# Sixteen-head cross attention: the order of the row tile groups on TensorE, and the bank that the weighed values are collected in

## The reference

```python
scores = jnp.einsum('bhqd,bhkd->bhqk', Q, K) / scale        # (8, 16, 100, 361)
attn = jax.nn.softmax(scores, axis=-1)
out = jnp.einsum('bhqk,bhkd->bhqd', attn, V)                # (8, 16, 100, 16)
out = out.transpose(0, 2, 1, 3).reshape(B, L, D) @ Wo + bo
```

## Time and profile before

| | us |
|---|---|
| median of three runs | 1513.96 |
| the profiled execution | 1514.17 |
| its span in the trace | 1512.4 |
| main loop of `l0x`, first to last turned maxima | 79.1 |
| the same of `l1x` | 79.6 |
| the same of `l3x` | 80.3 |

### The profile page before, as it was taken

One profiled execution on the slowest core, in us unless ns is written; L12 is line 12 of the kernel. 1 busy time (PEld: TensorE's weight loads), 2 busy tenths in 40 slices (PEclk: granted clock), 3 DMA queues, 4 the chain that ended last, 5 costly groups with the idle time before them and its releaser, 6 DMA issues. The chain is left out here.

```text
span 1512.4 us, 31527 instructions
## 1 busy us (share of the span) xinstructions
PE 1380.3 (91%) x12488; PEld 1067.8 (71%) x12488; DVE 777.7 (51%) x1733; ACT 644.3 (43%) x1683; POOL 194.8 (13%) x200
## 2 busy tenths in 40 slices
PE   7999899989989899899999889989958897899897
PEld 6776668866557588778999765669945676688632
DVE  3666677755556577520000466501127484576665
ACT  3444226643367356344444345432225674266300
POOL 3000250000024200040110420040042000300000
PEclk9999999999999999999999988999989995999999
DMA  6000340011301200366996100545221000700100
GB/s 214 2 1 1 68 68 16 3 43 42 79 8 21 47 9 3 105 230 246 340 345 247 48 22 1 202 186 200 73 55 37 1 2 1 112 9 3 67 1 22
DMA packets 43943, 120.19 MB, mean 79 GB/s; under 512 B 11931, under 2 KB 28440, under 8 KB 38412
## 3 DMA queue, kind: packets, MB, share of 16 engines
q1 hardware_dynamic: 33048, 62.04, 14.2%
q0 software_dynamic: 7616, 53.12, 10.1%
q10 hardware_dynamic: 3136, 3.03, 0.7%
HBM read 95.78 MB, written 11.00 MB: 71 GB/s over the span
## 5 line engine op out<-in xcount | busy, mean ns | idle before, releaser
L827 PE MATMUL wide<-early_kt,early_q 32*100 32x361 f32 x512 | 107.5, 507 | 2.8 <-PEq L66 1.6
L2558 ACT ACTIVATE l1f_hidden<-wide,l1f_pack 128x128 f32<-128x128 f32 x160 | 58.8, 368 | 78.0 <-PE wide L2497 68.1
L2680 DVE TENSOR_TENSOR l1f_out<-summed,l1f_pack 128x256 f32<-128x256 f32 x20 | 8.5, 424 | 152.9 <-PE summed L2505 152.9
L113 PE MATMUL summed<-ident 128*128 128x128 f32 x302 | 45.6, 319 | 33.3 <-PEq L66 33.3
L2497 PEld LDWEIGHTS wide<-l1f_rt,l1f_pack 128*128 128x128 f32 x640 | 74.5, 192 | 1.7 <-issue 0.8
L2497 PE MATMUL wide<-l1f_rt,l1f_pack 128*128 128x128 f32 x640 | 74.8, 275 | 0.6 <-ACT l1f_rt L2548 0.6
L2505 PE MATMUL summed<-l1f_pack,l1f_hidden 128*128 128x256 f32 x320 | 72.4, 379 | 0.0
L113 PEld LDWEIGHTS summed<-ident 128*128 128x128 f32 x302 | 43.3, 231 | 40.0 <-issue 40.0
L1223 DVE TENSOR_REDUCE l3x_mx<-wide 100x2 f32<-100x722 f32 x64 | 57.8, 907 | 14.7 <-PE wide L827 14.5
L1223 DVE TENSOR_REDUCE l1x_mx<-wide 100x2 f32<-100x722 f32 x64 | 57.8, 907 | 14.0 <-PE wide L827 14.0
L2505 PEld LDWEIGHTS summed<-l1f_pack,l1f_hidden 128*128 128x128 f32 x320 | 59.2, 190 | 7.2
(11 more groups left out here) (605 smaller groups left out, 3397.8 us busy)
## 6 DMA issues: line engine op xcount, KB each, us to landing
l2f_w<-l2f_w_dram SPq DMA_DIRECT2D x16, 1024.0 KB, 11.6
ctxt<-ctxt_dram SPq DMA_DIRECT2D x4, 1083.0 KB, 17.2
early_kt<-soon_kd SPq DMA_DIRECT2D x32, 90.8 KB, 3.3
l1f_sorted_x<-l1f_zeros SPq DMA_DIRECT2D x4, 640.0 KB
l1f_rows<-l1f_sorted_x SPq DMA_DIRECT2D x20, 128.0 KB, 7.7
l1f_sorted_y<-l1f_out ACTq DMA_DIRECT2D x20, 128.0 KB, 9.3
l0f_w<-l0f_w_dram SPq DMA_DIRECT2D x18, 128.0 KB, 2.1
l1f_shared<-l1f_shared_dram SPq DMA_DIRECT2D x1, 2180.0 KB, 8.2
```

Of the source, the lines that this page charges most:

```text
L113: pe.matmul(net.summed[:, 1, 0:P], net.ident[:], net.ident[:], start=True, stop=True)
L827: pe.matmul(wide[0:S, i, 0:SKV], q4[R * i:R * (i + 1), g % 2, b, g // 2, :], kt[R * i:R * (i + 1), g % 2, b, g // 2, 0:SKV], start=True, s ...
L2558: act.activation(hidden[:, f, 0:P], wide[:, f % 4, 0:P], ACT.Gelu, bias=b1_of(pack[:, n % SLOTS, :], f)).then_inc(sem["h_ready"], 1)
L2680: dve.tensor_tensor(out[:, n % 2], summed[:, n % 2, 0:E], b2_of(pack[:, n % SLOTS, :]), ALU.add).then_inc(sem["y_ready"], 1)
```

## The change

On TensorE, iteration n becomes: turned maxima of n; `score(n + 1, 1)`; `score_by_key(n - 1, (0, 1))`; `score(n + 2, 0)`; `score_by_key(n - 1, (2, 3))`; `weigh(n - 2)`. Both halves of the scores by key are now one quad behind, `weigh` stands last, and the mapping `TURN` is gone: turn i is head i. `weigh` writes into `scored[3]` instead of `scored[0]` and waits for the exponentials of its own quad only. On ScalarE `take(n - 1)` stands ahead of the fourth exponential of quad n instead of `take(n - 2)` behind the first. The turned maxima stay where they were, in bank 2 of `wide`.

```diff
-    TURN = (2, 3, 0, 1)
...
                     for c in range(NCH):
-                        for j in turns:
-                            i = TURN[j]
-                            last = pe.matmul(scored[j][0:CH, c * S:(c + 1) * S], kt[R * i:R * (i + 1), g % 2, b, g // 2, c * CH:(c + 1) * CH],
+                        for i in turns:
+                            last = pe.matmul(scored[i][0:CH, c * S:(c + 1) * S], kt[R * i:R * (i + 1), g % 2, b, g // 2, c * CH:(c + 1) * CH],
                                              q2[R * i:R * (i + 1), n % 2, :], start=True, stop=True)
                             if c == NCH - 1:
-                                last.then_inc(t_psum[j % 2], 1)
+                                last.then_inc(t_psum[i % 2], 1)
                 def weigh(n):
-                    pe.wait_ge(sem["p_ready"], min(Q * (n + 1) + 1, Q * QUADS))
+                    pe.wait_ge(sem["p_ready"], Q * (n + 1))
...
-                        for j in range(Q):
-                            i = TURN[j]
-                            last = pe.matmul(scored[0][i * V:(i + 1) * V, LOW:LOW + S], v1[0:rows_of(c), b, c, (Q * g + i) * W:(Q * g + i) * W + V],
-                                             pt[0:rows_of(c), (Q * n + j) % 8, c, :], start=c == 0, stop=c == NCH - 1)
+                        for i in range(Q):
+                            last = pe.matmul(scored[3][i * V:(i + 1) * V, LOW:LOW + S], v1[0:rows_of(c), b, c, (Q * g + i) * W:(Q * g + i) * W + V],
+                                             pt[0:rows_of(c), (Q * n + i) % 8, c, :], start=c == 0, stop=c == NCH - 1)
...
                     if 1 <= n <= QUADS:
+                        score_by_key(n - 1, (0, 1))
+                    if n + 2 < QUADS:
+                        score(n + 2, 0)
+                    if 1 <= n <= QUADS:
                         score_by_key(n - 1, (2, 3))
                     if n >= 2:
                         weigh(n - 2)
-                    if n + 2 < QUADS:
-                        score(n + 2, 0)
                     if n == 0:
                         keep_busy(pe, net, 3)
-                    if n < QUADS:
-                        score_by_key(n, (0, 1))
...
-                    act.activation(sums[:, n // NQ, n % NQ, :], scored[0][:, LOW:LOW + S], ACT.Copy).then_inc(sem["sums_ready"], 1)
+                    act.activation(sums[:, n // NQ, n % NQ, :], scored[3][:, LOW:LOW + S], ACT.Copy).then_inc(sem["sums_ready"], 1)
...
-                for n in range(QUADS + 2):
+                for n in range(QUADS + 1):
                     if n < QUADS:
-                        exps(n, (0,))
-                    if n >= 2:
-                        take(n - 2)
+                        exps(n, (0, 1, 2))
+                    if n >= 1:
+                        take(n - 1)
                     if n < QUADS:
-                        exps(n, (1, 2, 3))
+                        exps(n, (3,))
```

## The result

The changed kernel took 1497.61 us (median of four executions, 1495.78 to 1500.19), the kernel before, beside it on the same chip, 1513.81 (1509.19 to 1515.53): a ratio of 0.9896 with a 95% interval of 0.9858 to 0.9934. That is 16.2 us less; 14.3 were forecast, and 1499.7. Run again against 24 executions of the kernel before, it gave 0.9918 (0.9889 to 0.9947), 1497.66 us. The time is where it was expected. The trace says that it did not come from where it was expected throughout: two of the three loops gained nearly what was forecast, the third gained nothing, and two stages that the change does not touch made up for it.

What follows compares the result with a forecast made beforehand. PE's own list sets the pace: 2.534 us a quad falls to 2.37, 0.164 times 29 quads is 4.8 us a loop, three loops 14.3, ends cancelling: 1514.17 - 14.3 = 1499.9, or 1499.7 from the median; range 1495 to 1509.

Steps and rivals of the forecast that it cites:

- PE's list: TensorE's work per quad: turned maxima 0.23, both halves 1.48, weighing 0.65, together 2.36 us, 2.47 at the upper end.
- the pattern that iteration 1 had shown: In the kernel before, iteration 1 lacks a weighing; the next half's weights load 0.65 after the half before began, not 0.82.
- the wait for `highest(n + 1, 0)`: `score(n + 2, 0)` waits between the halves for VectorE's maxima, due at 0.86 to 0.90; row groups come free at 0.88.
- The three loops that are close: Loops of waits per quad on PE, DVE and ACT: 2.36, 2.34 and 2.30 us; 2.37 taken, 0.01 above the longest.
- VectorE's loop: DVE's way from one turned maxima to the next, through `with_maxima` and `highest`: 2.34 us a quad.
- The ends: Start and end of each main loop: 0.92 us gained, 0.92 lost, set off with 0.5 us either way.
- The third loop: The loop of `l3x`: 4.8 us gain like the others; its existing delays left as they are, 1 us in the range.
- A: Rival: a wait halves the gain, by PE's upper end or a longer ACT loop; 6 to 8 us, 1506 to 1508; chance 0.14.
- ScalarE's loop: ACT's loop through `take`, fourth exponential, scores by key and weighing: 2.30 us a quad, reserve 0.06 against PE's.
- B: Rival: row groups do not run past one another, a quad stays 2.53, nothing is gained, 1514 us; chance 0.08.
- C: Rival: second-half scores by key wait in program order; quad 2.81, 24 us more, 1538 us; chance 0.08.
- the 1.07 that the prediction names: Start of scores by key for (2, 3) after the turned maxima from which C decides; 0.92 to 1.01 was expected.

Runs made afterwards that it cites:

- halves apart: The changed kernel with the turned maxima put between the two halves, all else as changed: 1514.06 us, 1.0004 against the kernel before.
- VectorE out of the way: The changed kernel with VectorE's maxima taken over the first 181 of 361 keys only: 1491.26 us, 0.9831 against the kernel before.
- the wrong bank: The changed kernel with the weighing put back into `scored[0]`, with the waits that this needs: 1520.51 us, 1.005 against the kernel before.
- keys after eight quads: The changed kernel with SP issuing the last key transfers of `l3x` only after the scores of eight quads: 1498.88 us, 0.9883.
- keys ahead: The changed kernel with keys of batches 2 and 3 issued before queries in `l3x`, their tiles cleared earlier: 1504.4 us, then 1494.4 us.
- two copies: The changed kernel with ScalarE's `take` cut into two copies of 64 partitions each: 1529.96 us, 1.013 against the kernel before.

## Why the prediction was right, and where it was not

- **PE's list**: the mechanism is right, and the number is in part luck. 0.23 + 1.48 + 0.65 was forecast, 0.23 + 1.47 + 0.65 measured (1.50 in every other quad), in the pattern that iteration 1 had shown. With the halves apart it is 2.54 again. But with VectorE out of the way the halves take 1.43: PE's list alone is 2.32 or less, and what makes it 2.35 to 2.39 is the wait for `highest(n + 1, 0)`, of which the prediction said "No cost, and no reserve".
- **The three loops that are close**: 2.36, 2.34 and 2.30 were forecast; PE's list is 2.32 or less, VectorE's loop 2.35, ScalarE's 2.31. So the longest is VectorE's. That the loops wait for one another now and then cost 0.012 to 0.018 more than my 0.01: 2.382 and 2.388 a quad, not 2.37, or 0.4 us a loop. This sits in the seven quads of 2.49 to 2.52, in which the two halves take 1.60 to 1.63; without them the mean is 2.37 in both loops.
- **The ends**: at the start the turned maxima of quad 2 follow those of quad 0 after 4.74 us instead of 5.62, 0.88 gained (0.92 forecast). At the end the last weighing ends 5.98 after the last turned maxima (6.07 forecast, 5.15 before), and the stage's last result comes 0.84 later, 19.83 instead of 18.99 after them. They cancel, as said. The rows, as the earlier trace rows:

```profile
218.72 0.30 PE L831 MATMUL wide<-ident,l0x_mx 100*128 100x100 f32 x1 [0.24 <-ACT l0x_v L982]
223.46 0.30 PE L831 MATMUL wide<-ident,l0x_mx 100*128 100x100 f32 x1 [0.63 <-DVE l0x_mx L1220]
...
292.55 0.30 PE L831 MATMUL wide<-ident,l0x_mx 100*128 100x100 f32 x1
298.53 1.08 PE L861 MATMUL wide<-ident,l0x_both 128*100 128x128 f32 x8
```

- **The third loop**: wrong. The step that failed is "The keys and queries that DMAs still bring are needed at most 14 quads x 0.16 + 0.92 = 3.2 us earlier", priced at nothing, with 1 us for single delays. I asked whether the data would be there, and it was. I did not ask what else those transfers hold up: PE's own instructions, due every 5 us or so, arrived so late that PE stood still for 3.4 us, and the clock was at 0.50 behind the stall. The forecast gain of 4.8 us came out as a loss of 1.0. A trace of before had the sign: a stall of 0.51 in front of "issue", in the loop with the highest DMA share (0.18 in the earlier trace rows). The prediction also took the start of the stage to stay as it was; the first projection of queries took 4.62 us instead of 2.92, at a granted clock of 0.63 instead of 1.00, and with it SP started the last keys 1.6 us later against the loop.
- **The sum**: 14.3 forecast; 15.7 and 12.4 measured by the two ratios, 16.2 by the medians of the first comparison. That it is so close is luck in part. In the traces the three stages gave 8.8 instead of 14.3, and 9.1 came from a clock that differs between executions of one kernel too. At a like clock it is 11 to 15. The range, 1495 to 1509, holds either. The 3 us that were to tell a change from none are too few: the two intervals are 9 to 12 us wide.
- **The rivals**: A (a wait for an exponential in each quad) did not come, ScalarE's loop of 2.31 stayed under VectorE's 2.35; B (nothing) is what the halves apart give, 1514.06. C (the second half held in program order, 1538) is refuted: scores by key of the second half start at 260.18, 0.92 after the turned maxima, ahead of the scores by query that stand earlier in the list (their first passes start at 260.22, their second at 260.53). In six of the seven long quads they start 1.02 to 1.06 after the turned maxima, just short of the 1.07 that the prediction names. By the rule of the Trainium skill, "TensorE: Matmul & The Clock Gate", Part 2, that matmuls keep program order, this could not be; for matmuls of different row groups the trace disagrees here, by 0.04 and 0.35, as it did before.

## What to carry to other kernels

When an engine is busy to the last hundredth, look at what each piece of its list waits for inside the array: two pairs of row groups that can run past one another are worth more side by side than with full-array work between them, here 0.15 us in 2.53. Before you count on it, add up the other engines' loops with the new order; here VectorE's had nothing to spare and ScalarE's some 0.05, and one copy more, or the wrong bank, made the kernel slower than before. Look at the instruction queue wherever a loop runs beside heavy transfers: what the transfers delay need not be data. And before a difference between two traces is put down to a change, compare the granted clock of the stages that the change leaves alone.

## What the runs showed of the hardware

- PE's instruction packets share the DMA engines with the kernel's transfers: 4.3 to 6.1 us apart in a quiet loop, 9.4 us beside key transfers. PE went on 3.0 to 3.3 us after the late packet in each of four traces (before, after, keys after eight quads, keys ahead).
- How long PE stood in front of the same packet did not go by its pace: 0.51 and 2.59 us at 2.53 a quad (before, halves apart), 3.43 at 2.38 (after), 2.29 at 2.70 (two copies).
- After 3.43 us of standing still PE ran at a granted clock of 0.50 for about 5 us; after 0.97 us, in the kernel with the keys ahead, it stayed at 1.00.
- A second copy on ScalarE right behind one cost 0.26, and an exponential behind the second one came 0.12 later than behind a single one.
- The same stage of the same instructions took 63.5 or 67.8 us, and another 181.8 or 188.0, at a granted clock of 0.97 or 0.90 and 0.87 or 0.82. One and the same kernel showed both lengths of the first.
